# Spline matmuls of a convolution kernel in eight 64x32 tiles instead of four 128x32 tiles

## What is computed

```python
def _L0_conv_ref(x, w1, gamma1, beta1, w2, gamma2, beta2):
    out = relu(_batchnorm(_conv3x3(x, sign(w1)), gamma1, beta1))
    out = _batchnorm(_conv3x3(out, sign(w2)), gamma2, beta2)
    return relu(out + x)

def _L1_conv_ref(x, a, b, alpha_table, mix, id_gain, bias):
    x_aff = clip(x * a[None, :, None, None] + b[None, :, None, None], -1.5, 1.5)
    u = (x_aff + 1.0) * 0.5 * (K - 1)
    i = floor(u); t = clip(u - i, 0.0, 1.0)
    i0, i1, i2, i3 = (clip(i + d, 0, K - 1) for d in (-1, 0, 1, 2))
    b0, b1, b2, b3 = _cubic_basis(t)
    spline = alpha_table[i0] * b0 + alpha_table[i1] * b1 + alpha_table[i2] * b2 + alpha_table[i3] * b3
    y_nl = einsum('bchwr,cr->bchw', spline, mix)
    return id_gain * x + y_nl + bias
```

## Time and profile before

| | |
|---|---|
| median of 3 runs | 1327.04 us (1324.48 to 1327.2) |
| the profiled execution | 1323.77 us |
| its span, first to last instruction | 1322.0 us |
| mean granted TensorE clock | 0.980 |
| both convolutions | from the start to about 440 us |
| spline, TensorE's part | 462.74 to 1314.32 us |

### The profile page before, as it was taken

One profiled execution on the slowest core, in us unless ns is written; L12 is line 12 of the kernel. 1 busy time (PEld: TensorE's weight loads), 2 busy tenths in 40 slices (PEclk: granted clock), 3 DMA queues, 4 the chain that ended last, 5 costly groups with the idle time before them and its releaser, 6 DMA issues.

```text
span 1322.0 us, 63361 instructions
## 1 busy us (share of the span) xinstructions
PE 1248.0 (94%) x29706; PEld 849.0 (64%) x29706; DVE 1003.8 (76%) x922; ACT 897.9 (68%) x357; POOL 59.0 (4%) x132
## 2 busy tenths in 40 slices
PE   6999994999999099999999999999999999999997
PEld 4677773678887056666667766666666666666664
DVE  5765564666665588888888888888888888888875
ACT  4354444678776268886888688867886788778860
POOL 5000000281000000000000000000000000000000
PEclk9999997999999599999999999999999999999999
DMA  6666665477767455665466555644565455545411
GB/s 222 239 260 262 255 244 199 176 275 273 264 254 295 137 158 149 179 165 128 149 182 156 133 148 175 161 136 148 170 162 139 148 168 161 143 148 160 123 43 51
DMA packets 53510, 235.94 MB, mean 178 GB/s; under 512 B 15808, under 2 KB 15808, under 8 KB 45248
## 3 DMA queue, kind: packets, MB, share of 16 engines
q1 hardware_dynamic: 52544, 231.18, 54.6%
q10 hardware_dynamic: 768, 1.61, 0.4%
HBM read 104.29 MB, written 77.07 MB: 137 GB/s over the span
## 4 chain that ended last, share of the span: by engine, by line
PE 64%; DVE 1%; ACTq 0%; ACT 0%; issue 0%; DVEq 0%
PE tab L991 64%; ACTq L804 0%; DVE zbuf L856 0%; DVE lin L850 0%; DVE poly L922 0%; DVE lin L935 0%; DVE mask L886 0%; ACT zbuf L788 0%; ACT cell L796 0%; DVE lin L862 0%; DVEq L921 0%; DVEq L849 0%
## 5 line engine op out<-in xcount | busy, mean ns | idle before, releaser
L991 PE MATMUL tab<-mask,diag 128*32 128x392 bf16 x20480 | 851.4, 329 | 22.8 <-DVE mask L886 22.7
L991 PEld LDWEIGHTS tab<-mask,diag 128*32 128x32 f16 x20480 | 546.5, 97 | 327.5 <-DVE mask L886 22.8
L818 ACT ACTIVATE mask<-cell,thr 128x6272 bf16<-128x6272 bf16 x93 | 509.2, 5507 | 2.0 <-PE tab L991 2.0
L922 DVE SCALAR_TENSOR_TENSOR poly<-tab,first,poly 128x1568 f32<-128x1568 f32 x93 | 172.1, 1851 | 102.9 <-PE tab L991 99.6
L637 PE MATMUL acc<-band_split,w 64*64 64x392 f16 x4608 | 197.9, 330 | 14.5 <-DVE band_split L427 13.3
L637 PE MATMUL acc<-split,w 64*64 64x392 f16 x4608 | 196.9, 330 | 14.4 <-DVE split L438 11.4
L354 ACT ACTIVATE yout<-acc 128x1568 f32<-128x1568 f32 x64 | 94.3, 1473 | 170.0 <-PE acc L637 170.0
L637 PEld LDWEIGHTS acc<-band_split,w 64*64 64x64 f16 x4608 | 159.1, 107 | 52.9 <-issue 18.7
L447 DVE BATCH_NORM_STATS2 stats<-yout 128x392 f32 (+1 forms) x256 | 126.0, 555 | 86.5 <-ACT yout L354 85.7
L637 PEld LDWEIGHTS acc<-split,w 64*64 64x64 f16 x4608 | 141.6, 107 | 68.9 <-issue 15.5
L788 ACT ACTIVATE zbuf<-lin,cst 128x1568 f32<-128x1568 f32 x32 | 54.3, 1697 | 175.3 <-DVE lin L850 169.7
(11 more groups left out here) (110 smaller groups left out, 377.5 us busy)
## 6 DMA issues: line engine op xcount, KB each, us to landing
y_scratch<-yout SPq DMA_DIRECT2D x32, 1568.0 KB, 6.2
cell<-cell SPq DMA_DIRECT2D x496, 98.0 KB, 3.7
xin<-y_scratch SPq DMA_DIRECT2D x16, 1568.0 KB, 9.1
zbuf<-y_scratch SPq DMA_DIRECT2D x32, 784.0 KB, 4.7
lin<-in_x SPq DMA_DIRECT2D x32, 784.0 KB, 9.0
out<-lin SPq DMA_DIRECT2D x32, 784.0 KB, 5.1
xin<-in_x SPq DMA_DIRECT2D x15, 1568.0 KB, 9.3
cell<-cell ACTq DMA_DIRECT2D x16, 98.0 KB, 3.0
```

The costliest lines, as they stand in the source:

```text
L818: act.activation(mask[b % 2][q][:, :, :], cell4[b % 2][:, :, :], ACT.Sign, bias=thr[:, q:q + 1]).then_inc(sign_mask_ready, 1)
L922: dve.scalar_tensor_tensor(out=quarters(poly), in0=summed(i, b, t), scalar=base(i, b, t), in1=quarters(poly), op0=ALU.add, op1=ALU.add).th ...
L991: mm = pe.matmul(tab[(b + t) % 2][j * GROUP:(j + 1) * GROUP, sub, 0:SUB], keep["diag"][part][:, j % 2, t, q, :], mask[b % 2][q][:, j, sub ...
```

## The change

The rows of a matmul now hold two thresholds instead of four (`TOGETHER` = 2), and the two halves of the 128 rows belong to two halves of the pixels. The groups g of `cell4` are thresholds g % 2 of the pixel half g // 2, so `cell4` and every mask are half as wide (`HALF` = 784 pixels). There are eight sets of two thresholds in place of four quads; VectorE makes two mask tiles per chunk, ScalarE six (before: one and three). A matmul contracts 64 rows, for one pixel half h and one channel group j; the eight pairs (h, j) are eight 64x32 tiles of the array. A table takes 8 sets x 2 quarters x 2 parts x 2 halves x 4 groups = 256 matmuls. `diag`, `thr` and `above` have eight sets. The number of cell copies stays (16 per chunk), each of half the size.

```diff
-QUADS = 4
+HALF = CHUNK // 2
+PIXEL_HALVES = 2
+TOGETHER = 2
+SETS = STEPS // TOGETHER
-SIGN_QUADS = (1, 2, 3)
-VECTOR_QUADS = (0,)
+SIGN_SETS = (2, 3, 4, 5, 6, 7)
+VECTOR_SETS = (0, 1)
...
-            for q in range(QUADS):
+            for q in range(SETS):
                 for g in range(4):
-                    above = SHIFT + 1 + 2 * (4 * q + g)
+                    above = SHIFT + 1 + 2 * (TOGETHER * q + g % TOGETHER)
                     link(pool.memset(thr[g * GROUP:(g + 1) * GROUP, q:q + 1],
-                                     0.5 - above if q in SIGN_QUADS else above))
+                                     0.5 - above if q in SIGN_SETS else above))
...
                 for half in range(2):
-                    for q in range(QUADS):
+                    for q in range(SETS):
                         for part, d in enumerate((dhi, dlo)):
                             link(pool.tensor_scalar(keep["diag"][part][:, half, t, q, :], ident4[:, :],
                                                     d[:, half, t, q:q + 1], None, ALU.mult))
...
-        cell4 = [sb(f"cell4{b}", [P, 4, CHUNK], BF16) for b in range(2)]
-        mask = [[sb(f"mask{s}{q}", [P, 4, CHUNK], BF16) for q in range(QUADS)] for s in range(2)]
+        cell4 = [sb(f"cell4{b}", [P, 4, HALF], BF16) for b in range(2)]
+        mask = [[sb(f"mask{s}{q}", [P, 4, HALF], BF16) for q in range(SETS)] for s in range(2)]
...
+        def pixels(g):
+
+            return slice(g // TOGETHER * HALF, (g // TOGETHER + 1) * HALF)
...
                         sp.dma_start(cell4[b % 2][g * GROUP:(g + 1) * GROUP, j, :],
-                                     cell[b % 2][j * GROUP:(j + 1) * GROUP, :]).then_inc(copied[b % 2], 16)
+                                     cell[b % 2][j * GROUP:(j + 1) * GROUP, pixels(g)]).then_inc(copied[b % 2], 16)
...
                 if following:
-                    sign_mask(i, b + 1, SIGN_QUADS[0])
+                    for q in SIGN_SETS[:2]:
+                        sign_mask(i, b + 1, q)
                 if after:
                     cells(i, b + 2)
                 if following:
-                    sign_mask(i, b + 1, SIGN_QUADS[1])
-                    sign_mask(i, b + 1, SIGN_QUADS[2])
+                    for q in SIGN_SETS[2:]:
+                        sign_mask(i, b + 1, q)
                     sides(i, b + 1)
...
-                    for sub in range(4):
+                    for sub in range(2):
+                        own = slice(sub * SUB, (sub + 1) * SUB)
                         for part in range(2):
-                            for j in range(4):
-                                mm = pe.matmul(tab[(b + t) % 2][j * GROUP:(j + 1) * GROUP, sub, 0:SUB],
-                                               keep["diag"][part][:, j % 2, t, q, :],
-                                               mask[b % 2][q][:, j, sub * SUB:(sub + 1) * SUB],
-                                               start=(q == 0 and part == 0),
-                                               stop=(q == QUADS - 1 and part == 1))
+                            for h in range(PIXEL_HALVES):
+                                rows = slice(h * TOGETHER * GROUP, (h + 1) * TOGETHER * GROUP)
+                                for j in range(4):
+                                    mm = pe.matmul(tab[(b + t) % 2][j * GROUP:(j + 1) * GROUP, 2 * h + sub, 0:SUB],
+                                                   keep["diag"][part][rows, j % 2, t, q, :],
+                                                   mask[b % 2][q][rows, j, own],
+                                                   start=(q == 0 and part == 0),
+                                                   stop=(q == SETS - 1 and part == 1))
```

More of the change, by code:

```diff
@@ L111, in convolutions @@
         halves = sb("halves", [P, TABLES])
[L112 to L115, removed]
+        dsel = sb("dsel", [P, 2, TABLES, SETS])
+        dhi16 = sb("dhi16", [P, 2, TABLES, SETS], F16)
+        dhi = sb("dhi", [P, 2, TABLES, SETS])
+        dlo = sb("dlo", [P, 2, TABLES, SETS])
         acc = ctx.enter_context(nc.psum_tensor("acc", [P, 2 * TILES, BANK], F32))
@@ L499, in steps @@
                                            ALU.subtract), chain)
-                    signed = step[:, l, :, 4 * SIGN_QUADS[0]:4 * SIGN_QUADS[-1] + 4]
+                    signed = step[:, l, :, TOGETHER * SIGN_SETS[0]:TOGETHER * (SIGN_SETS[-1] + 1)]
                     link(dve.tensor_scalar(signed, signed, 0.5, None, ALU.mult), chain)
-                signed = step[:, 0, :, 4 * SIGN_QUADS[0]:4 * SIGN_QUADS[-1] + 4]
+                signed = step[:, 0, :, TOGETHER * SIGN_SETS[0]:TOGETHER * (SIGN_SETS[-1] + 1)]
                 link(dve.tensor_reduce(halves[:, :], signed, AX.X, ALU.add), chain)
@@ L508, in steps @@
                         own = slice(g * GROUP, (g + 1) * GROUP)
-                        link(dve.tensor_copy(dsel[own, half, :, :], step[own, 1 + half, :, g:STEPS:4]), chain)
+                        link(dve.tensor_copy(dsel[own, half, :, :], step[own, 1 + half, :, g % TOGETHER:STEPS:TOGETHER]), chain)
                 link(dve.tensor_copy(dhi16[:, :, :, :], dsel[:, :, :, :]), chain)
@@ L718, in vector_masks @@
         def vector_masks(c):
-            return (c + 1) * len(VECTOR_QUADS) + len(SIGN_QUADS) if not isinstance(c, int) or c >= 0 else 0
+            return (c + 1) * len(VECTOR_SETS) + len(SIGN_SETS) if not isinstance(c, int) or c >= 0 else 0
         def sign_masks(c):
-            return c * len(SIGN_QUADS) if not isinstance(c, int) or c >= 0 else 0
+            return c * len(SIGN_SETS) if not isinstance(c, int) or c >= 0 else 0
+        def pixels(g):
+            return slice(g // TOGETHER * HALF, (g // TOGETHER + 1) * HALF)
         def exists(n, b):
@@ L877, in masks @@
                 wait_past(dve, table_ready, TABLES * (BUFS * i + b - 1))
-                for q in VECTOR_QUADS:
+                for q in VECTOR_SETS:
                     dve.tensor_scalar(mask[b % 2][q][:, :, :], cell4[b % 2][:, :, :], thr[:, q:q + 1], None,
@@ L884, in first_masks @@
                 dve.wait_ge(copied[0], COPIES)
-                for q in range(QUADS):
+                for q in range(SETS):
                     dve.tensor_scalar(mask[0][q][:, :, :], cell4[0][:, :, :], keep["above"][:, q:q + 1],
-                                      2.0 if q in SIGN_QUADS else 1.0, ALU.is_ge, ALU.mult).then_inc(mask_ready, 1)
+                                      2.0 if q in SIGN_SETS else 1.0, ALU.is_ge, ALU.mult).then_inc(mask_ready, 1)
             def base(i, b, t):
@@ L980, in table @@
                 wait_past(pe, table_used, TABLES * c + t - 1)
-                for q in range(QUADS):
+                for q in range(SETS):
                     if t == 0 and isinstance(c, int) and c == 0:
                         pe.wait_ge(mask_ready, q + 1)
-                    elif t == 0 and q in SIGN_QUADS:
-                        pe.wait_ge(sign_mask_ready, sign_masks(c - 1) + SIGN_QUADS.index(q) + 1)
+                    elif t == 0 and q in SIGN_SETS:
+                        pe.wait_ge(sign_mask_ready, sign_masks(c - 1) + SIGN_SETS.index(q) + 1)
                     elif t == 0:
-                        pe.wait_ge(mask_ready, vector_masks(c - 1) + VECTOR_QUADS.index(q) + 1)
-                    for sub in range(4):
+                        pe.wait_ge(mask_ready, vector_masks(c - 1) + VECTOR_SETS.index(q) + 1)
+                    for sub in range(2):
+                        own = slice(sub * SUB, (sub + 1) * SUB)
                         for part in range(2):
-                            for j in range(4):
-                                mm = pe.matmul(tab[(b + t) % 2][j * GROUP:(j + 1) * GROUP, sub, 0:SUB],
-                                               keep["diag"][part][:, j % 2, t, q, :],
-                                               mask[b % 2][q][:, j, sub * SUB:(sub + 1) * SUB],
-                                               start=(q == 0 and part == 0),
-                                               stop=(q == QUADS - 1 and part == 1))
+                            for h in range(PIXEL_HALVES):
[6 more added lines that the diff above has]
+                                                   stop=(q == SETS - 1 and part == 1))
                 mm.then_inc(table_ready, 1)
@@ L1022, in build @@
             "avg": sb("avg", [P, P]),
-            "thr": sb("thr", [P, QUADS]),
+            "thr": sb("thr", [P, SETS]),
             "first": sb("first", [P, TABLES]),
             "plain": sb("plain", [P, TABLES]),
-            "above": sb("above", [P, QUADS]),
+            "above": sb("above", [P, SETS]),
             "w": [[sb(f"w{n}_{i}", [P, TAPS * C], F16) for i in range(2)] for n in range(2)],
@@ L1033, in build @@
             "x_loaded": [sem(f"x_loaded_for_sum{b}") for b in range(BUFS)],
-            "diag": [sb(f"diag{i}", [P, 2, TABLES, QUADS, GROUP], F16) for i in range(2)],
```

(1 more changed line is left out.)

## The result

| | before | change |
|---|---|---|
| median | 1325.78 us (4 runs) | 1760.35 us (4 runs, 1754.73 to 1763.32) |
| ratio | | 1.3273, 95% interval 1.3232 to 1.3314 |
| profiled execution | 1323.77 us | 1762.4 us |
| span | 1322.0 us | 1760.6 us |
| mean granted clock | 0.980 | 0.949 |

The change is slower by a third. The forecast was 1610 us in a range of 1480 to 1770 us: the measured time lies inside, near its upper end.

The account below looks back on a forecast made before the run. TensorE's matmuls bound the spline; with twice the instructions, block delivery would. 1323.8 us plus 291 for delivery minus 0.9 at the start gave 1614, 1617 with the median, rounded to 1610 us; range 1480 to 1770.

Parts of the forecast that it names:

- the larger of run and trip per block: Spline: when a block comes too late, time per block is the larger of 2.65 us and the round trip.
- no block is asked for further ahead: TensorE's instruction supply: a block is requested only when the one before it begins to be used.
- the undelayed round trip: Spline instruction blocks: an undelayed fetch takes 2.7 us, between 2.2 and 3.2.
- The margin of 3.2 us: Kernel before, spline: an undelayed block arrives about 3.2 us early, out of the 5.3 us its predecessor lasts.
- the DMA's part: Spline chunks: loads delay blocks by 3.3 us, halved copies by 1.4 us, the store priced like the copies.
- Array work: Spline matmuls: eight half-height tiles take as long as four, 0 us, with up to 23 us kept for the range.
- Masks: Spline masks: ScalarE +0.8 us per chunk, VectorE at most +0.28 us, both hidden behind TensorE.
- Before the first matmul: Start of the spline: the first mask at half size takes 0.9 us less on the chain, -0.9 us.
- GpSimd: Second convolution: 160 slices instead of 80, 41 us more work, needed only at 462.7 us, so no cost.
- The supply keeps up: Rival for the spline: blocks arrive in time, TensorE's time stays 851 us, kernel 1326 or 1322 us; chance 0.12.
- The clock: Rival: TensorE's holes at chunk loads also drop its clock, +96 us, about 1710 us, or 2175 throughout; chance 0.10.
- A floor per pair: Rival: spline matmul pairs cannot go faster than 41.6 ns, +851 us, 2175 us, likelier near 1500; chance 0.08.

Follow-up runs that it names:

- experiment 1: The change with TensorE's spline program as a loop over two tables, 80 turns, always summing the first chunk's masks: 1340.99 us, ratio 1.0113.
- experiment 3: The kernel before, old tiles and masks, with two superfluous weight loads before every matmul's own, 512 instructions per table: 1832.25 us, ratio 1.3829.
- experiment 5: The kernel before with two superfluous weight loads per matmul, looped over two tables for 80 turns, later masks left out of the sum: 1347.66 us, ratio 1.0170.
- experiment 7: The change with spline loads and stores of 16 columns from chunk 4 on, cell copies from chunk 2 on, same number of issues: 1671.05 us, ratio 1.2596.
- experiment 8: The change with cell copies of 16 columns instead of 784 from chunk 2 on, loads and stores whole: 1743.84 us, ratio 1.3189.
- loads2: The kernel of experiment 3: the kernel before with two superfluous weight loads per matmul, written out without a loop: 1832.25 us, ratio 1.3829.

## Why the prediction was right, and where it was not

**What held.** The bound would move from the array to the delivery of instructions: shown from both sides, by the tiles without delivery (experiment 1, +15.6 us) and by the instructions without the tiles (experiment 3, +506 us, of which experiment 5 takes nearly all back). The blocks of 256 instructions, the bursts of 128 pairs, the larger of run and trip per block: seen in the timeline. That no block is asked for further ahead fits all runs, and in experiment 7 every transfer starts 1.0 to 2.0 us after the burst before it; how far ahead the hardware could ask wasn't tried by itself.

**The step that failed in size: the undelayed round trip.** I took 2.7 us between 2.2 and 3.2. It is 3.75 us (experiment 7), outside my bounds. The upper bound added 0.97 us of transfer, 1.65 us from its end to TensorE and a guess of 0.6 us before its start; measured are 1.11, 1.39 and 1.26 us, so the guess for the start was half of what it is. The margin of 3.2 us would have given more: it came out of 5.3 us plus what TensorE still had queued, a part that I named and did not add. The traces show its size. In the kernel before, counted on from 694.76 us in steps of 5.31 us, TensorE reaches new blocks at 705.4 and 710.7 us, and the transfers of the blocks behind them start at 705.1 and 710.1 us, 0.3 and 0.6 us earlier; in experiment 7, where nothing is queued, they start 1.26 us later. So 1.5 to 1.8 us of work were queued, and 5.3 + 1.5 - 3.2 = 3.6 us or somewhat more is the trip. The Trainium skill ("TensorE: Matmul & The Clock Gate", Architectural detail: the array is 16× 32×32, not 1× 128×128) gives TensorE a queue of 64; at 5.32/256 us per instruction that is 1.3 us and the trip 5.3 + 1.3 - 3.2 = 3.4 us, an estimate; the trace agrees roughly, with 1.5 us or more.

**The step that failed the other way: the DMA's part.** My 35.7 us per chunk held 10 x 2.7 = 27 us of undelayed trips and 8.7 us of delay. Measured are 37.5 and 2.8 us: 1290 us / 32 = 40.3 per chunk, less 10 x 3.75. That is about what the loads alone were given (0.8 blocks by 3.3 us). The copies were the mistake: I halved their delay because their bytes halve (2.4 blocks by 1.4 us, 3.4 us per chunk), and it all but vanished: 17 us over 32 chunks in experiment 8, 0.5 us each. At full size they do seem to delay: loads2, with the same number of instructions and copies of 98 KB, takes 72 us more than the change, of which the extra weight loads explain some 7 (experiment 5); no run of loads2 with small copies shows the rest to be theirs. So the delay is probably not in proportion to the bytes: before, the DMA engines were 90% busy while the copies ran, in the change 64% (888.0 to 899.5 us). The two errors were of opposite sign and only partly cancelled, so the total fell 150 us short. That the measured time lies inside the range is in part luck: with the right trip of 3.75 us and the delays as I had them, a chunk would have come to 44.7 us and the kernel to some 1900 us, outside it. As shares of the 439 us: 320 x (3.75 - 2.66) = 349 us come from undisturbed trips, 320 x (4.03 - 3.75) = 90 us from those that traffic delays.

**Array work, 0 to 23 us.** Zero is right: in experiment 1 the 40960 matmuls were busy 866.9 us, 15.5 more than before, and 79 turns of 0.2 us, the same price as with the old tiles in experiment 5, account for nearly all of it.

**Masks.** ScalarE's went from 5507 to two of 2893 ns, +0.84 us per chunk (forecast +0.8); VectorE's from 1845 to two of 1028, +0.21 us (at most 0.28). Both hidden, as said.

**Before the first matmul.** Forecast -0.9 us. The chain of the change where the spline begins:

```profile
460.60 0.96 DVE mask L894
461.56 0.04 issue
461.60 8.53 PE tab L1002 x273
```

The mask takes 0.96 instead of 1.77 us, and the stage starts 1.1 us earlier. ScalarE's copies of half the size still go out at 0.62 us each.

**GpSimd.** Busy 103.0 us instead of 59.0, and nothing waits for it.

**The rivals.** *The supply keeps up*: refuted by the looped kernels of experiments 1 and 5 against their written-out ones. The Trainium skill ("Runtime: NRT & Kernel Launch", Instruction fetch mechanics) calls the crossing between blocks mostly hidden. This case agrees at 5.3 us per block, and disagrees at 2.65, where an undisturbed crossing costs 1.1 us on average (3.75 - 2.65). *The clock*: it did fall, the sign that I had named for this rival. These are windows of the change:

```profile
520.00:1750.00 1230.00, 914.74 (x39025) 599.19 (x39025) 685.20 (x447) 623.27 (x262) 0.00 (x0) 0.95 0.25 78
927.00:937.00 10.00, 5.54 (x172) 2.83 (x162) 5.44 (x4) 10.00 (x5) 0.00 (x0) 0.70 0.60 189
```

The lower level follows the long holes at the loads. But it costs little: the 10.64 us burst from 932.77, after such a hole, holds three blocks without a gap, and the next burst begins 11.51 us after it did, 3.84 us per block, hardly more than an undisturbed trip. While TensorE is slow, the next block comes in. All 28 bursts of two or three blocks together take 263 us for 65 blocks, 4.04 us each, at most 19 us above 3.75, against 96 us that the rival asked. This is read from the trace; no run kept the clock up with the loads in place. *A floor per pair*: refuted. Experiment 1 keeps up 866.9 us / 40960 = 21.2 ns per pair. The Trainium skill ("TensorE: Matmul & The Clock Gate", Wait — 56ns, not 53.3ns?) states that starts are never closer than about 25 ns; for matmuls in eight different tiles the runs disagree, and with them the 1500 us of that rival.

None of the kernels measured beats the kernel before. The array needs some 851 us for this sum in either tiling, and the kernel before already gets nearly all its instructions in time.

## What to carry to other kernels

Before cutting matmuls into smaller tiles, divide the run time of a stage by its instructions: what counts is how long 256 of TensorE's own, weight loads included, keep it busy. Here 5.3 us was safe, 4.7 us cost 2% of the kernel's time, 3.5 us 14% and 2.65 us a third, while a loop whose 64 KB body was already there ran at 2.65 us per 256 with only 0.2 us per turn of 1024 instructions. Short idle times marked "issue", evenly spaced and with a fixed number of instructions between them, are this.

## What was not expected

- An undisturbed trip of an instruction block takes 3.75 us on average with the DMA engines 4% busy, and mostly has one of three lengths that lie 0.27 us apart.
- Two superfluous weight loads per matmul are nearly free where instructions are at hand: 1347.66 against 1340.99 us with as many loop turns.
- A fall of the clock to its lower level after holes of 4 us costs little when the stage waits for instructions anyway: at most some 19 of 439 us by the change's trace.
